# Digits of one-hot steps read from a PSUM bank instead of from SBUF, with three banks for the moves of a sort

## What is computed

```python
edge_index = jnp.stack([src, dst])
x = _layernorm(x + L0(x, edge_attr_2, src, dst, ...))   # attention over the edges of each dst, with moments of z[src], z[dst]
x = _layernorm(x + L1(x, edge_index))                   # sum of x[src] over the edges of each dst
x = _layernorm(x + L2(x, edge_index, edge_attr_16, ...))# attention over each src, then a GRU cell
x = _layernorm(x + L3(x, src, dst, W, b))               # attention over the edges of each dst
```

## Time and profile before

| | us |
|---|---|
| median of three runs | 11759.01 (11755.06 to 11760.62) |
| the profiled execution | 11769.89 |
| its span | 11768.2 |
| POOL busy | 8350.4 |
| DVE busy | 5629.5 |
| ACT busy | 2619.6 |
| PE busy | 2530.8 |

### The profile page before, as it was taken

How to read it: one execution, slowest core, us unless ns; L and a number is a source line. 1 busy time by engine, 2 the same in 40 slices (tenths; PEclk the granted TensorE clock), 3 DMA queues, 4 the chain that set the end, 5 groups by cost and what they waited for, 6 DMA issues and landing times. The chain is left out here.

```text
span 11768.2 us, 56949 instructions
## 1 busy us (share of the span) xinstructions
PE 2530.8 (22%) x12070; PEld 2016.1 (17%) x12070; DVE 5629.5 (48%) x13769; ACT 2619.6 (22%) x3769; POOL 8350.4 (71%) x8546
## 2 busy tenths in 40 slices
PE   2322434320200000000000001666666640000000
PEld 2211323220200000000000000555555530000000
DVE  9999898970422222421111112677777542222223
ACT  1155555540111111112222220111111121111111
POOL 0077777777777777667777777777777657777776
PEclk8555555555555555555555555787888755555555
DMA  7000000011222222211111111333333212222222
GB/s 223 11 14 13 13 14 14 7 28 32 58 55 55 55 54 55 52 52 53 53 51 53 53 52 46 86 87 86 86 88 87 59 27 55 53 55 55 55 54 49
DMA packets 689050, 631.35 MB, mean 54 GB/s; under 512 B 453662, under 2 KB 511671, under 8 KB 687681
## 3 DMA queue, kind: packets, MB, share of 16 engines
q0 software_dynamic: 273056, 240.52, 10.7%
q1 hardware_dynamic: 414782, 380.90, 10.0%
q10 hardware_dynamic: 864, 6.29, 0.1%
HBM read 322.26 MB, written 304.83 MB: 53 GB/s over the span
## 5 line engine op out<-in xcount | busy, mean ns | idle before, releaser
L1202 POOL DMA_INDIRECT l_rows<-table,l_sources x4704 | 4477.1, 952 | 1474.8 <-issue 1433.4
L606 POOL DMA_INDIRECT e_rows<-in_rec,base x1568 | 1668.6, 1064 | 1059.8 <-DVE marks L733 579.0
L1202 POOL DMA_INDIRECT l_pair<-table,l_slab x1568 | 1505.1, 960 | 483.5 <-issue 459.6
L1401 DVE TENSOR_TENSOR_SCAN l_totals<-l_factor,banks 128x510 f32<-128x510 f32 (+3 forms) x672 | 752.8, 1162 | 1677.1 <-ACT banks L1556 1675.9
L1566 ACT COPY l_kept<-l_totals 128x476 f32<-128x476 f32 (+3 forms) x672 | 639.2, 967 | 3191.5 <-DVE l_totals L1401 3181.9
L1332 DVE TENSOR_TENSOR l_score<-l_rows,base 128x14 f32<-128x14 f32 x224 | 41.3, 185 | 2672.0 <-DMA l_rows<-table,l_sources 2672.0
L1518 PE MATMUL banks<-ident,l_kept 128*65 128x128 f32 (+2 forms) x4 | 1.9, 463 | 5865.0 <-DVE junk L1450 5865.0
L1518 PEld LDWEIGHTS banks<-ident,l_kept 128*65 128x65 f32 (+2 forms) x4 | 0.7, 170 | 5866.8 <-DVE junk L1450 5866.8
L751 PE MATMUL banks<-marks 125*128 125x98 bf16 x3200 | 623.3, 366 | 1235.3 <-DVE marks L733 1235.3
L388 DVE COPY_PREDICATED area<-banks,area 128x2048 f32<-128x2048 int32 x342 | 869.0, 2596 | 0.2
L751 PEld LDWEIGHTS banks<-marks 125*128 125x128 bf16 x3200 | 460.3, 148 | 1386.2 <-DVE marks L733 1282.0
(11 more groups left out here) (310 smaller groups left out, 6302.7 us busy)
## 6 DMA issues: line engine op xcount, KB each, us to landing
l_rows<-table,l_sources POOLq DMA_INDIRECT x4704
sums<-l_kept SPq DMA_DIRECT2D x112, 476.0 KB
sums<-l_kept SPq DMA_DIRECT2D x224, 231.0 KB
sums<-l_kept SPq DMA_DIRECT2D x112, 462.0 KB
seeds<-zeros SPq DMA_DIRECT2D x130, 392.0 KB
sums<-l_kept SPq DMA_DIRECT2D x112, 448.0 KB
l_pair<-seeds SPq DMA_DIRECT2D x224, 224.0 KB, 3.3
e_rows<-in_rec,base POOLq DMA_INDIRECT x1568
```

The costliest lines, as they stand in the source:

```text
L606: GP.indirect_dma_start(e_rows[:, u, g, :], None, A["rec16"], bass.IndirectOffsetOnAxis(e_ids[:, s * G16 + g:s * G16 + g + 1], 0)).then_in ...
L1202: GP.indirect_dma_start(pair[:, u, g, 0:D] if gated else rows[:, u, g, :], None, table[l], bass.IndirectOffsetOnAxis(at, 0)).then_inc(rows ...
L1401: V.tensor_tensor_scan(flat(totals[:, s % 2, h, 0:n, :]), flat(factor[:, s % 2, 0:n, :]), flat(fresh[s % 2][h][:, 0:n, :]), 0.0, ALU.mult, ...
```

## The change

The digits of a step are no longer read from SBUF. They are copied into bank 4 as f32, 16 steps at a time (256 edges for each of the two digits), and the step reads them there. The copy is done by DVE before the first step of each 16 and before step 24, and waits for DVE's last one-hot. Bank 4 is thereby taken from the moves of both sorts, which turn over three banks, 5 to 7.

```diff
@@ sort_tensor
-                        bank = ps[4 + used % 4]
-                        if used >= 4:
-                            pe.wait_ge(s["kept"], used - 3)
+                        bank = ps[5 + used % 3]
+                        if used >= 3:
+                            pe.wait_ge(s["kept"], used - 2)
@@ hist_vector
+        HELD = 16
+        held = ps[4][0:EP, :].rearrange("p (j c) -> p j c", j=2)
+
         def hist_vector(dve):
 
             def one(i):
                 k, s = "ds"[i // HSTEPS], i % HSTEPS
                 h, summed = hist[k]["hot"], hist[k]["summed"]
+                if s % HELD == 0 or i == BEGUN:
+                    a = s // HELD * HELD * HC
+                    n = min(HELD * HC, EK - a)
+                    if i:
+                        dve.wait_ge(*hist["ds"[(i - 1) // HSTEPS]]["hot"].done((i - 1) % HSTEPS))
+                    link0(dve, V.tensor_copy(held[:, :, 0:n], digit[k][:, :, a:a + n]))
                 if i >= HOTS:
                     dve.wait_ge(*(summed.done(s - HOTS) if s >= HOTS else hist["d"]["summed"].done(i - HOTS)))
                 for j, n in ((0, P), (1, NB)):
                     V.tensor_tensor(hot[j][0:EP, i % HOTS, 0:n, :], count_j[0:EP, 0:n, :],
-                                    digit[k][:, j, None, s * HC:(s + 1) * HC].to_broadcast([EP, n, HC]),
+                                    held[:, j, None, s % HELD * HC:(s % HELD + 1) * HC].to_broadcast([EP, n, HC]),
                                     ALU.is_equal).then_inc(h.sem, 1)
```

## The result

| | before | after |
|---|---|---|
| median of 6 runs | 11757.03 (11749.90 to 11762.34) | 11806.33 (11798.98 to 11810.58) |
| ratio | | 1.0043 (1.0031 to 1.0054) |
| the profiled execution | 11769.89 | 11808.01 |
| its span | 11768.2 | 11806.3 |
| DVE busy | 5629.5 | 6009.1 |

The change makes the kernel 49 us slower (the two medians). The two profiled executions lie 38 us apart. The prediction had said 72.

The account below looks back on a forecast made before the run. The stage was taken to end with POOL's last gather, behind sort "s" on DVE, with DVE's side in slack. A start 139 us late less 67 us of holds given back made +72 us: 11831 us, range 11787 to 11882.

Parts of the forecast that it names:

- The path: Order that sets the stage's end: sort "s" on DVE, then POOL's 1568 gathers, then flags and moments, then layer 0.
- The step: One-hot step on DVE: reading f32 digits from PSUM costs 1.90 us more per step, bounds nothing and 2.6 us.
- The first gather: POOL's first gather, behind sort "s": starts about 38 us later.
- Step 76 and group 58: One-hot step in sort "d" ends 142 us later; the gather group needing it starts 139 us late, then no more waits.
- the refills: The 15 DVE copies of digits into bank 4: 0.85 us each, two in sort "s", four up to step 76.
- The waits for the pace: POOL's gather groups waiting for set one-hot steps on DVE: from some 20 to some 150 us within the stage.
- The holds: POOL's gather issues lengthened while DVE instructions read two SBUF tensors: 67 of 130 us given back, bounds nothing or 90.
- Three banks: Moves of both sorts turning over three banks for four: nothing lost.
- DVE's slack: Some 283 us before the block closes; DVE's side would be ready at about 2883 us, POOL's last gather at 2947.
- The read that isn't slower: Rival: one-hot steps stay at 2.1 us and holds go, -65 us, 11694 us; chance 7%.
- the hold that stays: Rival: the PSUM read holds POOL's issues as before, and longer, +306 us, 12065 us; chance 7%.
- DVE as the bound: Rival: at about 3 us more per step DVE's side meets POOL's, +155 us, 11914 us; chance 3%.

Follow-up runs that it names:

- e11: Changed kernel, but the 24 steps inside sort "s" read bf16 digits from SBUF, with refills and bank reads only from sort "d" on; 11781.5 us, ratio 1.0005.
- e6: Changed kernel, but the digits lie packed as bf16 in bank 4, so no operand is 4 bytes wide; 13613.0 us, ratio 1.0156.
- e2: Changed kernel with its refills and three banks, but the steps read bf16 digits from SBUF as before; 13390.25 us, ratio 0.9998.
- e3: Changed kernel, but the held f32 digits lie in a tile in SBUF, not in bank 4; 13405.44 us, ratio 1.0003.
- e1: Kernel before with only the banks of the moves changed, three for four, digits still read from SBUF; 13401.25 us, ratio 1.0012.
- e8: The changed kernel word for word, measured again in the third series beside the kernel before at 13399.02 us; 13737.09 us, ratio 1.0256.
- e5: Kernel before without the pace, so gathers no longer wait for one-hot steps; 14463.43 us, ratio 1.0805.
- e9: Kernel before with a tighter pace: gather groups ask for later one-hot steps and 46 groups come after the sort; 13570.11 us, ratio 1.0117.

## Why the prediction was right and wrong, point by point

The sign, the place and the mechanism were right, the size was too large: 49 us where 72 stood, 19 us above the lower end of the range. No luck was needed: the errors below nearly all go the same way. (The range itself was not drawn evenly: its lower end adds both bounds below the forecast, 72 - 15 - 23 = 34; both above it would make 147 us and not 120.)

- **The path** (sort "s", then POOL's gathers, then the block's end) is shown by e11, in which the start alone was moved back by 36 us and the last gather came 32 us earlier, and by the sum below.
- **The step**: 1.90 us forecast, 1.87 measured. The nearest rows had the operand's width in common, and e6 shows that it is the width: 1214 ns with a 2-byte operand from the bank, 2279 with a 4-byte one from the bank, 2282 with a 4-byte one from SBUF. The table of the Trainium skill, "VectorE: DVE Perf Modes", section "The perf-mode tier table", has any operand in PSUM take tensor_tensor to one element a cycle; that gives the same sum for this change, but e6 contradicts it for a 2-byte operand. The text below that table limits only f32 in PSUM to one, and this fits e6.
- **The first gather**: +38 forecast, +39.1 measured (605.7 us after 566.6).
- **Step 76 and group 58**: +142 and +139 forecast, +136.5 and +133.2 measured. What is behind the first gather took 97.4 us and not 104. The first gather already waits for one of the 53 steps and for one refill, so 52 steps (97.2 us) and three refills (2.1 us) are behind it, and L382 took 2.5 us less; DVE's idle time there is 10 us in both kernels. The rest of the difference lies in the step (1.87 for 1.90) and in the refills: those of sort "s" delay the 24th step by 0.1 us in e2, where 1.7 had been added.
- **The waits for the pace** went from 22.5 to 153.8 us in the stage (about 150 forecast), counted over the usual 0.30 us in front of an issue; 48 groups waited at least 0.1 us more than that, instead of 5, the last of them group 58.
- **The holds** after group 58: 67 us given back forecast, 75.5 measured. The rule drawn from the timeline holds up: of the issues that were 0.13 us in while a step ran, 151 of 181 had been held before, and 0 of 430 were after. What was wrong is the split of the 130 us: in before the steps held 78.9 us from group 58 on and L367 45.2; in after L367 holds 50.9, and 57.4 us are left in all, where 63 were forecast. e3 shows that it is the pair of SBUF inputs that holds. The Trainium skill, "SBUF — State Buffer", section "Who interferes with whom", has such an instruction hold a GpSimd instruction that reads SBUF, not one that only writes it, and infers that the generation of descriptors isn't held. The prediction took from this that the page would have nothing given back. That was too quick: an issue of L606 reads its row numbers from SBUF (`e_ids`), and the hold, which catches an issue 0.13 us after its start, fits the first part. Whether the making of descriptors alone would be held, no run here shows.
- **The term that was missing**: POOL's 98 scatter issues (L574) were held as well. They stand between the gathers of groups 146 and 147, from 2221.6 us on in before, and it was the steps of sort "d" that held them (9.3 us). With the 0.30 us in front of each they took 140.7 us and now take 129.6, 11.1 us less. I had looked for held issues under L606 alone.
- **The sum**, with what was measured: 133.2 - 75.5 - 11.1 = +46.6, and the last gather is 46.4 us later. Of the 26 us by which the forecast of that gather (+72) was off, 6 lie in group 58, 9 in the holds and 11 in the scatter.
- **Three banks** at nothing, **the refills** at 0.85 us each: e1 and e2 show no cost in the total (1.0012 and 0.9998), but their intervals of 0.2% to either side, some 30 us, are too wide to settle it, and the stage is otherwise disturbed there. For the moves of sort "s" the end of the 24th step settles it (490.7 us in both). For those of sort "d" no total does, but they lie on DVE's side, which has slack, and the sum above closes within 0.2 us without them.
- **DVE's slack**: its side was forecast ready at 2883 us; the last store is issued at 2868.5 and POOL's last gather at 2921.7. Some 53 us are left of 283, and DVE's wait before L656 is 75 us (about 90 forecast).
- **Rivals.** The read that isn't slower fell with L742's 2279 ns, the hold that stays with its issues of 0.94 us, DVE as the bound with its 53 us of slack. But e8 shows that this last one is nearer than the 3% said: where PE waits under "issue", DVE's side does set the end, and the change costs 2.6%. Nothing in the trace of before shows such a wait.

What stays open: why the kernel before took 13390 us in three series and 11775 in another on a chip of those three; what holds PE in those series; and what a fast step without holds (e6) would be worth where PE has no such waits. The 65 to 80 us that its expectation names are argued and not shown.

## What to carry to other kernels

Look for a DMA issue that lasts longer than its siblings and read what another engine does in that moment: here 1.51 us against 0.95 under one kind of instruction gave away a cost of 133 us that no wait shows. Moving an operand can take such a cost away. Here it was the wider type, and not the new place, that made the instruction longer, and a longer instruction is worth it only where it isn't ahead of the engine that it should help. And where work of one engine starts a long queue on another, price the start first: the 36 us in front of the first gather went through to the end, while the 144 us more that the steps behind step 76 came late went into slack.

## What the runs showed of the hardware that I had not expected

- In some series PE and ACT stand idle for nothing that the profile shows while POOL issues indirect DMAs closely: PE 688.7 us at its step matmuls in e1 (270 times, up to 28.5 us) and 1773.1 us in e5, where POOL issued without the pace. In e5 it was 497.8 us in 566 us of dense issues and 22.2 us in the 569 us in which POOL stood still. In e3, whose POOL was held for 333 us, the step matmuls have none, but those at L909 behind the sort have 369.9 us. In those series the gathers of layer 0 came every 1.45 us instead of 1.27. Neither the two kernels of the result nor e11 in the fourth series show it at the steps, though POOL issues without a break there too, and e8 is the changed kernel word for word.
- Thinning the issues in one stage moves these waits to the next: 155.7 us at the steps, and 392.5 us at L899 behind them (e9).
- tensor_tensor over bf16 is as fast with one operand from PSUM as with both from SBUF, if that operand is packed bf16 (1214 ns for 2048 elements and 963 for 1568, where SBUF alone gave 1217 and 970), and the copy that puts such digits there as whole 4-byte words takes 0.43 us for 256 words, where the cast to f32 takes 0.695 us for 512 values.
